# Idle columns by the filled share of a trailing stretch, in place of idle columns in every planned gap of TensorE

## What is computed

```
x = x + causal self-attention(layernorm(x))            16 heads of 16
x = x + cross-attention(layernorm(x), ctx)             77 context rows of 192
x = x + top-2 of 8 linear experts(layernorm(x))
x = x + RNN(layernorm(x))       h_t = tanh(xi_t + h_(t-1) Wh^T + bh), t = 0..1023, 256 wide
x = x + cross-attention(layernorm(x), ctx)             other weights, with biases
x = x + gated experts (16 in 4 groups, top 4, and a shared one)(layernorm(x))
```

## Time and profile before

| | us |
|---|---|
| median of 3 runs | 1333.67 (1330.45 to 1336.44) |
| the profiled execution | 1336.98, its span 1335.2 |
| mean granted clock | 0.968 |
| first and last tanh of the RNN (L575), start | 204.7 and 1215.4 |

### The profile page before, as it was taken

The page is one execution under the profiler, slowest core; times in us unless marked ns, Lnnn a source line. Parts: engine busy times, 40 slices in busy tenths (PEclk is TensorE's granted clock), DMA queues, the critical chain, the costliest instruction groups (busy, mean ns, idle before and its releaser), DMA issues.

```text
span 1335.2 us, 48515 instructions
## 1 busy us (share of the span) xinstructions
PE 1291.6 (97%) x19651; PEld 894.3 (67%) x19651; DVE 857.7 (64%) x2733; ACT 626.6 (47%) x2842; POOL 88.5 (7%) x156
## 2 busy tenths in 40 slices
PE   5799999999999999999999999999999999999998
PEld 3465446777766777776677777766767677766555
DVE  7875587268777228787843257667755754566486
ACT  2163313844434783543467866543344455433322
POOL 2110100001000000100000010100000000000100
PEclk9799789999999999999999999979999999989999
DMA  6544300001000001100000023100000100001100
GB/s 192 123 124 149 65 1 2 22 15 44 3 3 5 13 9 41 42 3 3 2 27 3 4 99 108 39 3 2 2 2 19 50 3 3 18 2 35 32 1 17
DMA packets 52288, 44.48 MB, mean 33 GB/s; under 512 B 12203, under 2 KB 51302, under 8 KB 52070
## 3 DMA queue, kind: packets, MB, share of 16 engines
q1 hardware_dynamic: 47398, 40.39, 10.4%
q10 hardware_dynamic: 1600, 0.79, 0.3%
q0 software_dynamic: 3072, 0.21, 0.1%
HBM read 25.81 MB, written 15.15 MB: 31 GB/s over the span
## 4 chain that ended last, share of the span: by engine, by line
PE 92%; DVE 4%; DMA 1%; issue 1%; ACT 1%; SPq 0%; DVEq 0%; ACTq 0%
PE b L532 23%; PE b L1708 10%; PE b L1478 7%; PE b L1072 6%; PE b L549 6%; PE b L1043 5%; PE b L1778 5%; PE b L983 5%; PE b L714 4%; PE b L1336 3%; PE b L1311 3%; PE b L762 2%; PE b L473 2%; PE b L63 2%; PE b L666 2%; PE b L518 2%
## 5 line engine op out<-in xcount | busy, mean ns | idle before, releaser
L532 PEld LDWEIGHTS b<-hp,whp 128*128 128x128 f16 x12276 | 476.6, 96 | 244.1 <-ACT hp L575 160.6
L532 PE MATMUL b<-hp,whp 128*128 128x2 f16 x12276 | 533.2, 165 | 1.4 <-DVE hp L581 0.5
L581 DVE TENSOR_TENSOR hp<-hist,hp 128x4 f16<-128x4 f32 x1023 | 165.0, 161 | 340.8 <-ACT hist L576 328.1
L575 ACT ACTIVATE hp<-b 128x4 f16<-128x4 f32 x1024 | 177.6, 173 | 433.1 <-PE b L532 422.5
L992 DVE TENSOR_REDUCE mx<-b 128x1 f32<-128x512 f32 (+3 forms) x304 | 194.0, 654 | 2.5 <-PE b L986 1.7
L1057 ACT ACTIVATE vp<-b 128x512 f32<-128x512 f32 x288 | 170.9, 604 | 40.5 <-PE b L1046 26.6
L576 ACT ACTIVATE hist<-b 128x4 f32<-128x4 f32 x1024 | 178.9, 175 | 0.0
L1708 PE MATMUL b<-vp,heads 128*128 128x512 f16 x576 | 167.6, 386 | 0.0
L983 PE MATMUL b<-heads 128*128 128x512 f16 (+3 forms) x384 | 112.0, 335 | 5.5 <-DVE mx L992 3.4
L549 PE MATMUL b<-whp 128*128 128x512 f16 (+7 forms) x431 | 112.3, 332 | 0.0
L1478 PE MATMUL b<-we,xT 128*128 128x512 f16 x384 | 111.5, 383 | 0.0
(11 more groups left out here) (236 smaller groups left out, 1654.0 us busy)
## 6 DMA issues: line engine op xcount, KB each, us to landing
x_qs<-qx_scr SPq DMA_DIRECT2D x64, 96.0 KB
qx_scr<-xq_pair SPq DMA_DIRECT2D x16, 256.0 KB, 2.1
heads<-q_scr SPq DMA_DIRECT2D x32, 96.0 KB
heads<-k_scr SPq DMA_DIRECT2D x12, 192.0 KB, 4.7
x<-in_x SPq DMA_DIRECT2D x8, 256.0 KB, 6.7
q_scr<-tail SPq DMA_DIRECT2D x8, 256.0 KB, 2.3
k_scr<-tail SPq DMA_DIRECT2D x8, 256.0 KB, 2.3
x_qs<-in_L_ffn_We SPq DMA_DIRECT2D x2, 1024.0 KB, 5.6
```

Source lines behind the costliest of these rows:

```text
L532: return pe.matmul(self.z(t)[:, m], self.w.whp[:, a, k, m * P:(m + 1) * P], self.g.hp16[:, (t - 1) % 2, part, k, :], start=False, stop=Tru ...
L575: act.activation(self.g.hp16[:, t % 2, 0], self.z(t), ACT.Tanh, scale=1 / LIFT).then_inc(self.s["hi_ready"], 1)
```

## The change

`Kind` gets a field `full`: how much of an instance's planned time counts as filling the array (default: its whole cost). `hi` counts nothing, `lo` 0.21 us if it carries a heavy piece and else nothing, self values 0.6 of 0.7 us, cross scores 0.56 of 0.23, cross values 0.37 of 0.7, the gates of the linear experts and the logits of the gated ones nothing. The plan keeps a list of what was filled when, the idle columns included. Before each PE instance it works out `short`: 0.40 x 3.4 us less what was filled in the last 3.4 us of the plan. Where that is over 0.1 us it writes `short` us of idle columns. Before a `hi` it does so also where there is no gap, or a smaller one, and then moves `hi` later in the plan; before anything else the idle columns are no more than the gap.

```
-BURST_STEPS = 1024
-BURST = 1.7
+WINDOW = 3.4
+FULL_SHARE = 0.40
...
+        self.full = full if callable(full) else lambda i: full * cost(i)
...
+        def short_of(at):
+
+            while full and full[0][0] < at - WINDOW:
+                full.pop(0)
+            return FULL_SHARE * WINDOW - sum(us for _, us in full)
...
                 gap = at - free[e] if last_chain and by_name["hi"].next else 0.0
-                if gap > LEAST_GAP or burst(k) > LEAST_GAP and by_name["hi"].next:
-                    if gap > LEAST_GAP:
-                        run[0] = free[e]
-                    more = burst(k) if gap <= LEAST_GAP else max(0.0, BURST - gap) * (burst(k) > 0)
-                    at += more
-                    self.order[e].append(("idle", int((max(gap, 0.0) + more) * FULL_CLOCK // 64) * 64))
-                elif gap > 0.05:
-                    run[0] = at
-                if k.chain:
-                    run[0] = at + cost
+                short = short_of(at) if last_chain and by_name["hi"].next else 0.0
+                if k.name != "hi":
+                    short = min(short, gap)
+                if short > LEAST_GAP:
+                    at += max(0.0, short - max(gap, 0.0))
+                    full.append((at, short))
+                    self.order[e].append(("idle", int(short * FULL_CLOCK // 64) * 64))
...
+            if e == "pe":
+                full.append((at, k.full(i)))
...
-        st.add("pe", "hi", self.hi, S - 1, 0.213, lambda i: rank, chain=lambda i: 0.226)
+        st.add("pe", "hi", self.hi, S - 1, 0.213, lambda i: rank, chain=lambda i: 0.226, full=0.0)
...
-               chain=lambda i: 0.49, behind=[("hi", lambda i: i + 1)])
+               chain=lambda i: 0.49, behind=[("hi", lambda i: i + 1)], full=lambda i: 0.21 * self.heavy(i + 1))
```

More of the change, by code:

```diff
@@ L163, with __init__ @@
 class Kind:
-    def __init__(self, engine, name, count, cost, rank, after, opens=None, closes=None, chain=None, behind=None):
+    def __init__(self, engine, name, count, cost, rank, after, opens=None, closes=None, chain=None, behind=None, full=1.0):
         self.engine, self.name, self.count, self.cost, self.rank, self.after = engine, name, count, cost, rank, after
         self.opens, self.closes, self.chain, self.behind = opens, closes, chain, behind
+        self.full = full if callable(full) else lambda i: full * cost(i)
         self.next, self.waits, self.ready = 0, None, None
@@ L213, in make @@
         last_chain = None
[L214 to L220, removed]
+        full = []
         def ready_at(k):
@@ L246, in make @@
                 due = expected(e) if guarded else None
-                more = max((burst(k) for k in by_engine[e] if k.next < k.count), default=0.0)
                 for k in by_engine[e]:
@@ L264, in make @@
                         late = self.late if by_name["tanh"].next < HURRY else HURRIED
-                        slack = max(late + max(0.0, at - k.ready - PATIENCE) * 0.1, more)
+                        slack = late + max(0.0, at - k.ready - PATIENCE) * 0.1
                         if at + cost > due + slack:
                             continue
-                    key = (at, 0 if k.chain and not burst(k) else 1, k.rank(k.next))
+                    key = (at, 0 if k.chain else 1, k.rank(k.next))
                     if best is None or key < best[0]:
@@ L906, in __init__ @@
                opens=lambda n: ("self", self.blocks[n][0] // B) if self.blocks[n][0] % B == 0 and self.blocks[n][1] == 0
-               else None, behind=[("self_turn_o", lambda n: self.blocks[n][0] // B - 1)])
+               else None, behind=[("self_turn_o", lambda n: self.blocks[n][0] // B - 1)], full=0.6)
         self.merge = Merge(st, "self", [(c, w) for c in range(NK)],
@@ L1126, in __init__ @@
         st.add("pe", name + "_scores", self.scores, 2 * len(self.units), 0.23, lambda i: of_unit(i // 2) + 0.3,
-               opens=lambda i: (name + "s", i), behind=[(name + "_values", lambda i: i // 2 - 1)])
+               opens=lambda i: (name + "s", i), behind=[(name + "_values", lambda i: i // 2 - 1)], full=0.56)
         st.add("act", name + "_exp", self.exp, 2 * len(self.units), 0.52, lambda i: of_unit(i // 2) + 0.31,
@@ L1131, in __init__ @@
                opens=lambda u: (name, u // B) if u % B == 0 else None,
-               behind=[(name + "_turn_o", lambda u: u // B - 1)])
+               behind=[(name + "_turn_o", lambda u: u // B - 1)], full=0.37)
         self.merge = Merge(st, name, [(c, w) for c, w, _ in chunks], lambda u: (s["pv"], B * (u + 1)), rank, room.merge)
@@ L1361, in __init__ @@
                opens=lambda j: ("lin_gates", j // TC) if j % TC == 0 else None,
-               behind=[("n4_turn", lambda j: TC * (j // TC + 1))])
+               behind=[("n4_turn", lambda j: TC * (j // TC + 1))], full=0.0)
         st.add("v", "lin_route", self.route, S_ * NK, lambda i: 0.35 if 2 <= i % S_ < 7 else 0.2,
@@ L1537, in __init__ @@
                opens=lambda j: ("gat_logits", j // TC) if j % TC == 0 else None,
-               behind=[(ln.name + "_turn", lambda j: TC * (j // TC + 1))])
+               behind=[(ln.name + "_turn", lambda j: TC * (j // TC + 1))], full=0.0)
         st.add("act", "gat_ex", self.exp, n, 0.25, r(0.07), closes=lambda c: ("gat_logits", c))
```

## The result

The change made the kernel slower: 1347.41 us median of 18 runs (1337.06 to 1365.57) against 1336.14 for the kernel before on the same chips; the ratio is 1.0074, with a 95% interval of 1.0047 to 1.0101. The forecast was 1325.0, the range 1314 to 1339.

What follows compares the result with a forecast made beforehand. PE, busy 97%, and the RNN's step length were taken as the bound, with the tanh chain deciding in 501 of 1023 steps. Terms -10.7 + 6.5 - 4.5 = -8.7 us gave 1325.0 from the median 1333.67; range 1314 to 1339.

Steps and rivals of the forecast that it cites:

- The clock term: Within the RNN, half-clock falls at 878, 929 and 1168 (34.1 us) go: 10.7 us gained, bounds 8.5 and 15.2.
- The slower rival: Removed gap columns covered other stretches, where the clock now falls; 1341 us with three new falls of 17.07; chance 0.13.
- Removed columns: Idle columns trimmed from gaps in the RNN and behind it: 4.5 us gained, between 0 and 13.
- Added columns: Idle columns before `hi` without a gap, in 32 RNN steps: 8 us, 6.5 paid, bounds 3 and 10.
- The moved order: From the first `hi` set later, near 330 us, every engine's order may change: taken as 0, 4 us kept either way.
- the chance of faster: For the whole kernel, the chance of a time under 1327.0 us, given as 0.48.
- the clock follows something else than filled columns and the falls stay: Rival: the RNN's three falls stay, only the price and small gain are left, 1335.7 us; chance 0.10.
- The rule of the Trainium skill: Mid-kernel clock drops are avoided by leaving no long idle gaps between matmuls; by it, columns added without a gap couldn't matter.
- price and reordering eat the gain: Rival: 8 to 10 us paid for added columns, 8.5 given back, or reordering at its worst; about 1331; chance 0.22.

Runs made afterwards that it cites:

- e1: The changed kernel in its own order with each planned gap filled whole again, the columns added before `hi` kept; 1327.83 us, ratio 0.9964 to the kernel before.
- e4: The kernel before in its order with whole gaps, plus columns before `hi` up to 0.40, plan not moved; 1326.92 us, ratio 0.9952.
- e2: The kernel before in its order with gap columns trimmed to 0.40 and nothing added before `hi`; 1360.74 us, ratio 1.0188.
- e9: The kernel before in its order, gaps trimmed to 0.40 and columns added before `hi` to 0.40, plan not moved; 1348.00 us, ratio 1.0101.
- e8: As e4, but gaps filled up to a share of 0.60 in place of whole; 1330.25 us, ratio 0.9969 to the kernel before.
- e11: As e4, but each added piece before `hi` twice as long beyond its gap; 1333.95 us.
- e5: The kernel before in its order with no idle columns at all; 1394.50 us, ratio 1.0471.
- e3: The changed kernel with a wanted share of 0.50 in place of 0.40; 1350.26 us, ratio 1.0146 to the kernel before.
- e6: The changed kernel with a wanted share of 0.45 in place of 0.40; 1353.59 us, ratio 1.0170 to the kernel before.
- e12: As e4, with planned gaps ahead of the RNN filled too, once the weights the idle products read are there; 1323.39 us, ratio 0.9910.

## Why the prediction was wrong, step by step

**The clock term had the wrong sign, and it is nearly all of the error.** The sum had -10.7 us for three falls gone. Between the two profiled executions, 28.6 us apart, half clock makes +29.2 us (40.1 lost in 126.2 us, against 10.9 in 34.1 at 0.32 each), the rest of the RNN +0.4, the tail +3.0 and the earlier start -4.0; the medians are 11.3 us apart, with less half clock. The premise was one sentence: "The changed plan holds 0.40 there". It holds 0.40 of the last 3.4 us of the plan, by planned costs, and I took this as good for every place, while the earlier trace rows only showed that the light places without cover fall and that those with whole gaps don't. Nothing in the trace of before showed a covered place with its cover cut to 0.40. That is what the kernel has now, and there it falls. It also falls at two of the three old places, and the prediction had those as gone: at tanh 687 and 978 the additions alone don't hold the clock. With the same order and the same additions, but whole gaps around them (e1), they do. All eight falls begin at, or within 4 us of, places that the prediction had listed as short of columns: the steps at which they begin ran at 344, 533, 546, 595, 845, 885, 1033 and 1171 us in the kernel before. In e4, with the additions and without the trimming, the term is right: all three falls gone, and the kernel is 7.6 us faster than the one before on the same chip (1334.48); its RNN is 7.3 us shorter.

**The slower rival was the right case, under-priced.** It named the mechanism (gap columns as cover of stretches where the chain is alone) and the price per microsecond (0.31, measured 0.32). Its example, the stretch of 1134.9 to 1168.3, was not the place: no fall begins there in the changed kernel, and the clearest case came at 1047. It had three new falls of 17.07 us with the old ones gone; in the profiled run there were six new and two old ones, up to 30.7 us long, and it got a chance of 0.13 and lay mostly outside the range. The argument against it was the stretch of the earlier trace rows at about 0.4 with its clock at 1.00. In the changed kernel the clock fell at 846.0, four steps ahead of that very place, though with the work around it in another order; in e2 and e9, with the order of before, that place kept its clock. One stretch near a level that is itself counted by planned costs is thin evidence, and it was the evidence on which the chance hung.

**Removed columns: about right, and small.** The prediction had 3.5 us for the RNN. Reckoning 0.32 us for each of half clock, the RNN of before is 1010.7 - 10.9 = 999.8 us, that of e2 1045.3 - 49.1 = 996.2: 3.6 us for all trimmed gaps. That agreement hangs on the price: at 0.30 it would be 1.3 us. So between 1 and 4 us were won there. The reading of the earlier trace rows, that columns before a tanh-bound `hi` are free, holds: e8 trims 22 us of them for nothing. Behind the RNN the prediction took 1.0 (bound 4.8). In the changed kernel the tail is 122.8 us against e1's 123.7 with the same order, 0.9 less; in the order of before it is 116.5 in e2 against 119.8, 3.3 less.

**Added columns: right in kind, priced too high.** The prediction took 6.5 of 8 us as paid. In e4 the RNN is 1003.4 against 999.8, 3.6 us for 6.9 us of planned additions, about half. e11 measures 6.7 us for the next 7.3. The two differ because twice as long a piece no longer finds the little room that the first found, as at the earlier trace rows; that reason is argued and not shown.

**The moved order: 0, as taken**, at a share of 0.40, but as a sum of two parts: against e4, e1 has 2.0 us less in the RNN (1001.4 and 1003.4) and 3.9 more behind it (123.7 and 119.8). That is why the changed kernel's tail grew. The prediction was also wrong on where the order begins to differ: not near 330 us but at the second step, where the changed kernel has two idle products right before `hi` (L548 at 201.87) and the kernel before has none (`hi` at 205.88). At 0.45 the tail is 20 us longer than in the kernel before, which the kept 4 us would not have covered.

**The chances.** By its own parts (three quarters of 0.55 and a fifth of 0.22) the chance of faster was 0.46, not 0.48. That changes nothing in the outcome.

**The other rivals.** That the clock follows something else than filled columns and the falls stay is refuted by e4 and e5. The rule of the Trainium skill ("TensorE: Matmul & The Clock Gate", "Why this matters for your kernels"), which asks only that there be no long gaps between matmuls, doesn't tell these kernels apart: in the 4 us ahead of each of the changed kernel's eight falls PE stands for 0.27 us at most at a time, and the difference between e1 and the changed kernel is in what fills such short waits. That price and reordering eat the gain is what e3 and e6 do, but not the change.

**What stays open.** Why some runs of the same kernel have many falls and others few (1337.06 to 1365.57 us) wasn't tried. Part of the scatter lies ahead of the RNN, where all kernels but e12 do the same: their profiled runs have 23.9 to 51.2 us at half clock there, and the RNN starts at 196.2 us with the least and at 205.2 with nearly the most. Nor was it tried why a fall of the changed kernel lasts longer (20.5 to 30.7 us, the four long ones) than those of before (17.1 at most). A likely reason is that at half clock a step takes 1.3 us instead of 0.9, so that columns meant for a span of the plan are spread over a longer real one.

## What to carry to other kernels

Filler work that lies in a wait costs little: here 55 us of it cost 1 to 4 us within the RNN and 3.3 behind it. Cutting it saves no more than that and can cost the clock of everything around it, so take cover away only where a trace shows it to be paid. A rule that both trims and adds should be tried as two changes: here the one lost some 20 us and the other, without it, won 8. And if a plan keeps a level by planned costs, the level needs room above the point that was seen to matter, in the places where adding is free and not in all of them.

## What the runs showed of the hardware that was not expected

- The clock falls to 0.50 with PE at work: in the 4 us ahead of the fall at 340.8 it is busy for 4.00 us (the line below, of the changed kernel), and ahead of all eight falls it stands for 0.27 us at most at a time.
- What fills waits of 0.2 to 0.4 us decides over it: with the same order of work, half clock within the RNN is 0 us with whole gaps and 126.2 us with trimmed ones; with none at all, in the order of before, 262.6.
- A microsecond at half clock costs this kernel 0.32 us by the steps of e1 and the changed kernel, and not the 0.5 that work done at half speed would cost. In about half of the steps the weight load of `hi` waits for the tanh; that this is the reason is likely and not shown.

```profile
336.80:340.80 4.00, 4.00 (x80) 2.90 (x78) 1.44 (x7) 2.46 (x11) 1.03 (x2) 1.00 0.04 7
```
